# Head loop of a four-layer graph network: how reciprocal row sums reach all partitions

## What is computed

```python
def gat_layer(x, graph, W, b):
    h = x @ W
    s = jnp.einsum('bnd,bmd->bnm', h, h) * graph
    s = jnp.where(s == 0.0, NEG_INF, s)
    a = jax.nn.softmax(s, axis=2)
    return jnp.einsum('bnm,bmd->bnd', a, h) + b

heads = jax.vmap(lambda W, b: gat_layer(flow_x, graph, W, b))(Wh, bh)   # 8 heads of width 128
x = jax.nn.leaky_relu(cat, negative_slope=0.01)
out = gat_layer(x, graph, W_out, b_out)
```

## Time and profile before

| | us |
|---|---|
| median of 3 runs | 3390.68 |
| lowest and highest | 3390.52, 3391.51 |
| the profiled execution | 3389.07 |
| its span, first to last instruction | 3387.3 |
| the head loop within the span | about 350 to 2147 |

### The profile page before, as it was taken

The page is one execution under the profiler, slowest core; times in us unless marked ns, Lnnn a source line. Parts: engine busy times, 40 slices in busy tenths (PEclk is TensorE's granted clock), DMA queues, the critical chain, the costliest instruction groups (busy, mean ns, idle before and its releaser), DMA issues. The chain is left out here.

```text
span 3387.3 us, 48344 instructions
## 1 busy us (share of the span) xinstructions
PE 3089.4 (91%) x15547; PEld 1885.1 (56%) x15547; DVE 2982.4 (88%) x3851; ACT 2300.4 (68%) x3525; POOL 830.0 (25%) x580
## 2 busy tenths in 40 slices
PE   7998899999999999999999999799598888888857
PEld 3676566666666666666666666599554333333323
DVE  3578999999999999999999999688756999999944
ACT  0122677777777777777777777677346999999831
POOL 0123000000000000000000000000114999999921
PEclk9999999999999999999999999899799999999978
DMA  4000000000000000000000000000000000000001
GB/s 97 0 1 1 1 1 0 0 0 0 0 0 0 0 0 0 0 0 0 0 0 0 0 0 0 1 1 0 9 0 1 1 1 1 1 1 1 1 2 25
DMA packets 30364, 12.16 MB, mean 4 GB/s; under 512 B 27984, under 2 KB 29264, under 8 KB 30288
## 3 DMA queue, kind: packets, MB, share of 16 engines
q1 hardware_dynamic: 25056, 10.04, 1.3%
q10 hardware_dynamic: 5232, 1.12, 0.2%
HBM read 9.06 MB, written 2.10 MB: 3 GB/s over the span
## 5 line engine op out<-in xcount | busy, mean ns | idle before, releaser
L660 ACT ACTIVATE hid_work<-hid_work,hid_nmax 128x1024 f32<-128x1024 f32 x512 | 589.5, 1151 | 305.5 <-DVE hid_nmax L644 305.5
L632 DVE TENSOR_TENSOR hid_work<-hid_score_ps,A 128x1024 f32<-128x1024 f32 x512 | 618.3, 1208 | 30.0 <-PE hid_score_ps L593 29.9
L644 DVE CUSTOM_DVE_ANT_0 hid_work<-hid_masks,hid_work 128x1024 f32<-128x1024 f32 x512 | 620.6, 1212 | 0.2 <-DVE hid_masks L652 0.2
L1690 POOL TENSOR_TENSOR el<-el,node_edge 128x1024 f32<-128x1024 f32 x256 | 610.5, 2385 | 17.8 <-DVE el L1672 11.5
L671 ACT COPY hid_probsT<-hid_turn_ps 128x512 f32<-128x512 f32 x1024 | 542.2, 580 | 101.9 <-PE hid_turn_ps L607 101.9
L607 PEld LDWEIGHTS hid_turn_ps<-ident,hid_work 128*128 128x128 f32 x4096 | 458.4, 141 | 249.3 <-issue 206.0
L607 PE MATMUL hid_turn_ps<-ident,hid_work 128*128 128x128 f32 x4096 | 544.9, 276 | 4.9 <-ACT hid_probsT L671 3.9
L818 PE MATMUL hid_mix_ps<-hid_probsT,x_now 128*64 128x512 f32 x2048 | 497.2, 606 | 33.4 <-DVE hid_Zn L892 30.5
L592 PE MATMUL hid_score_ps<-hid_SX,hid_Y 128*128 (+1 forms) x1024 | 476.9, 466 | 2.6 <-DVE hid_SX L993 2.6
L593 PE MATMUL hid_score_ps<-hid_SX,hid_Yl 128*128 (+1 forms) x1024 | 405.5, 396 | 0.0
L1643 PE MATMUL spread<-hT_parts,pick 128*128 128x512 f32 x1024 | 309.2, 425 | 65.9 <-DVE u_buf L1666 61.6
(11 more groups left out here) (280 smaller groups left out, 4080.2 us busy)
## 6 DMA issues: line engine op xcount, KB each, us to landing
A<-in_adj_dram SPq DMA_DIRECT2D x4, 1024.0 KB, 9.8
X<-in_x_dram SPq DMA_DIRECT2D x8, 256.0 KB, 8.8
out_dram<-X SPq DMA_DIRECT2D x8, 256.0 KB, 3.4
wa<-in_L_gnn_weight_dram ACTq DMA_DIRECT2D x2, 256.0 KB, 15.2
wb<-in_L_gnn_weight_dram ACTq DMA_DIRECT2D x2, 256.0 KB, 13.6
wh<-in_L_gnn_Wh_dram SPq DMA_DIRECT2D x2, 256.0 KB, 5.5
incid<-in_L_gnn_H_dram SPq DMA_DIRECT2D x2, 256.0 KB, 3.5
wo<-in_L_gnn_W_out_dram SPq DMA_DIRECT2D x1, 256.0 KB, 6.1
```

The costliest lines, as they stand in the source:

```text
L632: nc.vector.tensor_tensor(work[:, kk % 4, :], score_ps[kk % 2][:], A[:, kk % NT, :], ALU.mult).then_inc(s["weighted"], 1)
L644: nc.vector.tensor_tensor_reduce(work[:, kk % 4, :], masks[:, kk % 2, :], work[:, kk % 4, :], -1.0, 3.0e38, ALU.add, ALU.min, nmax[:, kk % ...
L660: nc.scalar.activation(work[:, kk % 4, :], work[:, kk % 4, :], ACT.Exp, bias=nmax[:, kk % 4:kk % 4 + 1], scale=-1.0, accum_out=rowsum[:, k ...
L1690: nc.gpsimd.tensor_tensor(el[:, q % ELS, :], el[:, q % ELS, :], coefT[:, q // C, :], ALU.mult).then_inc(s_weighted, 1)
```

## The change

The R products, and with them ScalarE's copies from `misc_ps` to `rbc`, are left out: `EARLY` keeps only its W entries. Instead the SP queue runs a body per item with two transfers per group. The first stores the group's four columns of `rinv` to a DRAM tensor of 4 x 4 x 128 floats, so that the 512 values lie in the order of the rows; the second loads them from there into all 128 partitions of `rbc`. SP waits for the reciprocals, for the Zn that last read `rbc`, and for the store before it issues the load. `vec_norm` waits for the load instead of ScalarE's copy. `vec_invert` gets a wait for the store that last read the same columns of `rinv`, and a nop that carries the waits.

```diff
--- before.py
+++ after.py
@@ -708,6 +708,8 @@
             bh_now = sb("bh_now", [P, 1], F32, scope)
             x_now = sb("x_now", [P, 2, NT, C], F32, scope)
             rbc = sb("hid_rbc", [P, HALF], F32, scope)
+            r_rows = nc.dram_tensor("hid_r_rows", [4, GROUP, P], F32).ap()
+            r_stored, r_loaded = sem("hid_r_stored"), sem("hid_r_loaded")
             Zn = sb("hid_Zn", [P, 2, HALF], F32, scope)
             leaky = sb("leaky", [P, 2, 2, HALF], F32, scope)
             mix_ps, misc_ps = at.mix_ps, ps("hid_misc_ps", [P, HALF], scope)
@@ -717,8 +719,7 @@
             cleared = sem("hid_cleared")
 
 
-            EARLY = {0: ("R", 8), 2: ("W", 14), 4: ("R", 8), 6: ("W", 14), 8: ("R", 8), 10: ("W", 14), 12: ("R", 8),
-                     14: ("W", 14)}
+            EARLY = {2: ("W", 14), 6: ("W", 14), 10: ("W", 14), 14: ("W", 14)}
             LATE = {2: ("Y", 1, 0), 4: ("Y", 1, 1), 8: ("O", 0), 10: ("Y", 0, 0), 12: ("Y", 0, 1), 14: ("O", 1)}
 
             def group_of(i, k, lag):
@@ -763,19 +764,11 @@
                     return
                 pe.wait_ge(misc_read, use(i, k, False, first, last))
                 g, u, half, ib = group_of(i, k, EARLY[k][1])
-                if EARLY[k][0] == "R":
-                    pe.wait_ge(s["inverted"], g + 1)
-                    pe.nop(nofuse=True)
-                    for a in range(GROUP):
-                        slot = u * NT + half * GROUP + a
-                        done = nc.tensor.transpose(misc_ps[:, a * P:(a + 1) * P],
-                                                   at.rinv[:, slot:slot + 1].to_broadcast([P, P]), ident[:])
-                else:
-                    if u == 0 and half == 0:
-                        pe.wait_ge(staged_w, ib + 1)
-                    pe.wait_ge(s["normed"], g + 1)
-                    pe.nop(nofuse=True)
-                    done = nc.tensor.matmul(misc_ps[:], wh_now[:], Zn[:, half, :], start=True, stop=True)
+                if u == 0 and half == 0:
+                    pe.wait_ge(staged_w, ib + 1)
+                pe.wait_ge(s["normed"], g + 1)
+                pe.nop(nofuse=True)
+                done = nc.tensor.matmul(misc_ps[:], wh_now[:], Zn[:, half, :], start=True, stop=True)
                 done.then_inc(misc_made, 1)
 
             def pe_late(pe, i, k, first, last):
@@ -828,14 +821,8 @@
                 n = use(i, k, False, first, last)
                 g, u, half, _ = group_of(i, k, EARLY[k][1])
                 act.wait_ge(misc_made, n + 1)
-                if EARLY[k][0] == "R":
-                    if not first or g >= 1:
-                        act.wait_ge(s["normed"], g)
-                        act.nop(nofuse=True)
-                    nc.scalar.copy(rbc[:], misc_ps[:]).then_inc(misc_read, 1)
-                else:
-                    nc.scalar.activation(leaky[:, u, half, :], misc_ps[:], ACT.Identity,
-                                         bias=bh_now[:]).then_inc(misc_read, 1)
+                nc.scalar.activation(leaky[:, u, half, :], misc_ps[:], ACT.Identity,
+                                     bias=bh_now[:]).then_inc(misc_read, 1)
 
             def act_late(act, i, k, first, last):
 
@@ -879,6 +866,9 @@
                 g, u, half, _ = group_of(i, k, 6)
                 slots = slice(u * NT + half * GROUP, u * NT + (half + 1) * GROUP)
                 vec.wait_ge(s["exped"], GROUP * (g + 1))
+                if not first:
+                    vec.wait_ge(r_stored, 64 * i + 16 * ((k - 6) // GROUP) - 32)
+                    vec.nop(nofuse=True)
                 nc.vector.reciprocal(at.rinv[:, slots], at.rowsum[:, slots]).then_inc(s["inverted"], 1)
 
             def vec_norm(vec, i, k, first, last):
@@ -887,7 +877,7 @@
                     return
                 g, u, half, _ = group_of(i, k, 10)
                 vec.wait_ge(s["mixed"], g + 1)
-                vec.wait_ge(misc_read, use(i, k - 2, False, first, last) + 1)
+                vec.wait_ge(r_loaded, 64 * i + 16 * ((k - 10) // GROUP + 1))
                 vec.nop(nofuse=True)
                 nc.vector.tensor_tensor(Zn[:, half, :], mix_ps[:], rbc[:], ALU.mult).then_inc(s["normed"], 1)
 
@@ -955,11 +945,34 @@
                     pool.nop(nofuse=True)
                 stage_o(pool, bass.ds(i % HEADS, 1))
 
+            def sp_body(sp, i, first=False):
+
+                for d in range(4):
+                    sp.wait_ge(s["inverted"], 4 * i + d + 1)
+                    sp.nop(nofuse=True)
+                    sp.dma_start(r_rows[d].rearrange("a q -> q a"), at.rinv[:, d * GROUP:(d + 1) * GROUP],
+                                 allow_slow_non_contiguous=True).then_inc(r_stored, 16)
+                    if not first or d >= 1:
+                        sp.wait_ge(s["normed"], 4 * i + d)
+                        sp.nop(nofuse=True)
+                    sp.wait_ge(r_stored, 64 * i + 16 * (d + 1))
+                    sp.nop(nofuse=True)
+                    sp.dma_start(rbc[:], r_rows[d].rearrange("a q -> (a q)").unsqueeze(0).to_broadcast([P, HALF])
+                                 ).then_inc(r_loaded, 16)
+                    sp.wait_ge(r_loaded, 64 * i + 16 * (d + 1))
+                    sp.nop(nofuse=True)
+
             def x_bank(b):
 
                 return at.score_ps[b // 2 % 2][0:C, b % 2 * HALF:(b % 2 + 1) * HALF]
 
             block = scope.enter_context(nc.Block())
+
+            @block.sync
+            def _(sp):
+                sp_body(sp, 0, first=True)
+                with sp.Fori(1, ITEMS) as i:
+                    sp_body(sp, i)
 
             @block.gpsimd
             def _(pool):
```

## The result

| | us |
|---|---|
| after, median of 4 runs (3699.16 to 3706.72) | 3701.25 |
| before on the same chip, 4 runs | 3391.1 |
| ratio | 1.0921, 95% interval 1.0908 to 1.0935 |
| span of the profiled execution after | 3699.6 |

The account below looks back on a forecast made before the run. VectorE was taken as busy throughout the head loop but for one hole per item, closed in a cycle with TensorE. Removing R saves 32 x 0.35 = 11.2 us, all else zero: 3390.68 - 11.2 = 3379.5 us, range 3364 to 3396.

Parts of the forecast that it names:

- The store: SP's transfer of a group's 512 single reciprocals to DRAM: 3.0 us taken, between 2.2 and 5.7.
- the chain: From the reciprocal through both transfers to Zn's multiply: 6.9 us, bounds 5.7 and 12.1, hidden at no cost.
- The load: SP's transfer of the 2 KB row from DRAM into all 128 partitions: 3.6 us, bounds 3.2 and 6.1.
- The windows: Times from reciprocal to its Zn, four per item: 10.4, 11.0, 11.6 and 11.0 us; shorter transfers cost nothing.
- A: Rival: Zn on VectorE waits for late transfers, paying each window's excess; up to 157 us, about 3536; 12%.
- The rules on small writes: Skill rules against the store: one descriptor per element, read-modify-write below 512 bytes; the sum used trace rows instead.
- The fit: Skill's estimate for both transfers, 2.0 us plus bytes over 436 GB/s: 2.0 and 2.6 us, together 4.9, hidden.
- TensorE's stretch: Head loop, burst 7 to step 10's scores, no slack: removing step 8's R saves 0.35 us, 32 times, 11.2 us.
- C: Rival: VectorE's whole wait for scores in the head loop goes, 28.4 us, giving 3362.3 us; 12%.
- Contention and the nop: Transfer traffic, and VectorE's added wait and nop before each reciprocal: zero, upper bound 12.8 us for the nop.
- The end of the loop: Last reciprocal to last Zn, 7.15 us apart: the transfers just fit; zero, bounds -0.6 and +5.1 us.

## Why the prediction was wrong

- **The store: the step that failed.** The term was 3.0 us with 5.7 as the upper end. It measured 8.7 in the mean and up to 10.9. With it the chain came to 13.3 us in the mean, counted from the end of the reciprocal, where 6.9 was forecast and 12.1 was the upper bound, and it passed all four windows. The 3.0 was taken from the stores of X, 1024 runs of 256 bytes: none of those shares 64 bytes with another. The upper end, bh, has 1024 single elements, but on the reading side of DRAM; it was no bound for these writes. No row of before bounded the term from above, and the text said so ("no like in the trace") and used 5.7 all the same.
- **The load.** 3.6 expected, 4.7 measured, inside its bounds. It is 3.2 with spread stores and 3.9 with runs of 16 bytes. Behind the dense store it depends on that store: from the load's issue to Zn it is 4.8 us behind the 96 stores that took 8.3 in the mean, but 3.4 behind the 28 that took 10.2 (without the first item). Why the load is longer behind a dense store, and behind the shorter ones of them, even from another tensor, stays open.
- **The windows** held: 10.4, 11.0, 11.6 and 11.0 forecast with R gone, 10.26, 10.88, 11.56 and 11.03 measured without transfers. So did A's mechanism, and its price by the excess over each window: with the chain of 13.3 us the formula gives 32 x (3.0 + 2.4 + 1.9 + 2.4) = 310 against 323 by the table. Its price of 157 us was too low only because 12.1 was taken for the longest chain. A's chance of 12% was too small, since the sum hung on a term without a like.
- **The rules on small writes.** 512 writes of 4 bytes take 8.7 us side by side and 1.95 us when they are 256 bytes apart, so here their size and number alone don't decide. The rules of the Trainium skill, "DMA: Bandwidth & Descriptors" (Specifications; Rules for kernel authors), on transfers below 512 bytes and on single elements, which the prediction weighed and set aside, named the right part of the chain; they make no difference between these two stores. The fit that the prediction quotes from the same page of the Trainium skill is given there for transfers that GpSimd issues, and SP issued these.
- **TensorE's stretch.** The mechanism was right: one hole an item, shortened by R of step 8. The term was 0.35 us and is 0.40 by the two timelines; 11.2 us of gain were forecast for it, 13.3 are seen in VectorE's waits and 15 in the times. C, the whole hole, didn't come: 0.44 us are left.
- **Contention and the nop**: together 6 us by the kernel that doesn't wait, and 2.6 by the one with 256 bytes apart, where single runs of a kernel lie 3 to 5 us apart. Zero was forecast, with 12.8 as the bound.
- **The end of the loop**: from the last reciprocal to the last Zn it is 2447.14 - 2434.02 = 13.12 us, where it was 7.15. These 6.0 us lie above the bound of 5.1, by the same failed term; they are also most of what the change's last two columns differ by.

```profile
2434.02 0.17 DVE L872 RECIPROCAL hid_rinv<-hid_rowsum 128x4 f32<-128x4 f32 x1
2447.14 0.69 DVE L882 TENSOR_TENSOR hid_Zn<-hid_mix_ps,hid_rbc 128x512 f32<-128x512 f32 x1 [12.38 <-DMA hid_rbc<-hid_r_rows]
```

## What to carry to other kernels

A transfer inside a loop like this one, whose user waits in order on the engine that sets the pace, is free only up to the distance between its source and its user, and past that point it costs all of the excess in each round; work out that distance per use, and don't trust a duration that has no like in the trace. For a broadcast by way of DRAM, try the small store in few runs (here 1.73 us in place of 8.71), and put the order that this leaves right where a stepped access costs nothing, which here was TensorE's output.

## What the runs showed that was not expected

- Single 4-byte writes to DRAM: 512 side by side 8.7 us, 8 bytes apart 3.9, 64 apart 2.2, 256 apart 1.95; 128 runs of 16 bytes side by side 1.73. The dense store also has a second level near 10.3 us, in groups of two to four stores, with a group about every twelve stores.
- A read with a step of 16 bytes: VectorE 1053 for 678 ns; ScalarE 1153, for 603 from PSUM without a step. TensorE writing its output with that step: 605 ns as before.
- GpSimd's copy holds up VectorE's mask instruction: 19 ns in the mean, but about 1 us each in the seven cases where it began during a copy. The Trainium skill, "SBUF — State Buffer", Who interferes with whom, says that a `tensor_scalar` within SBUF can take the pair of ports that both engines share and that the later one is then blocked; the trace agrees: the mask that began 0.11 us behind a copy of 1.26 took 1.70, where 0.69 is usual.
